# Cross-attention and FFN on one core: the second group's attention in single precision, the stacked values built later

## The reference

```
x = x + xattn(layernorm(x), ctx)        # one head of width 512, 77 keys, masked softmax
x = x + ffn(layernorm(x))

xattn: Q = q @ Wq + bq;  K = c @ Wk + bk;  V = c @ Wv + bv
       scores = Q K^T / sqrt(512), masked keys -1e9;  attn = softmax(scores)
       return (attn @ V) @ Wo + bo
ffn:   real = x @ cos(theta + theta_noise);  imag = x @ sin(phi + phi_noise)
       return sqrt(real^2 + imag^2)
```

## Time and profile before

| | us |
|---|---|
| median of 3 runs | 254.1 (252.98 to 254.43) |
| the profiled execution's own time | 254.0 |
| its span, first to last instruction | 252.2 |
| PE busy | 236.2 (94%) |
| VectorE, ScalarE, GpSimd busy | 170.4, 145.1, 55.9 |
| mean granted clock of TensorE | 0.993 of full |

### The profile page before, as it was taken

The page is one execution under the profiler, slowest core; times in us unless marked ns, Lnnn a source line. Parts: engine busy times, 40 slices in busy tenths (PEclk is TensorE's granted clock), DMA queues, the critical chain, the costliest instruction groups (busy, mean ns, idle before and its releaser), DMA issues.

```text
span 252.2 us, 3916 instructions
## 1 busy us (share of the span) xinstructions
PE 236.2 (94%) x1249; PEld 134.9 (54%) x1249; DVE 170.4 (68%) x343; ACT 145.1 (58%) x251; POOL 55.9 (22%) x152
## 2 busy tenths in 40 slices
PE   7998698868699989999999999999999999999993
PEld 2898236326244457446744674467446744444462
DVE  1774759777796686678667966796579653965452
ACT  2301863459264934893579358925892589266542
POOL 1005053340073024202320332033103310132000
PEclk9999799999999999999999999999999999999999
DMA  6999958666227772597259726872877244424522
GB/s 198 374 413 415 417 144 160 65 155 271 63 44 209 133 322 48 125 224 299 65 147 208 312 42 196 160 308 44 219 142 307 42 83 83 169 42 83 188 107 83
DMA packets 48525, 44.80 MB, mean 178 GB/s; under 512 B 42518, under 2 KB 42774, under 8 KB 45309
## 3 DMA queue, kind: packets, MB, share of 16 engines
q1 hardware_dynamic: 47557, 43.37, 57.7%
q0 software_dynamic: 288, 1.05, 2.4%
q10 hardware_dynamic: 664, 0.18, 0.3%
HBM read 25.66 MB, written 8.39 MB: 135 GB/s over the span
## 4 chain that ended last, share of the span: by engine, by line
PE 68%; DMA 12%; DVE 9%; SPq 4%; issue 3%; ACT 2%; POOL 2%; DVEq 0%; ACTq 0%; POOLq 0%
DMA wo<-in_Wo 8%; PE im L486 7%; PE re L486 7%; PE im L488 7%; PE re L488 7%; PE re L487 7%; PE im L487 7%; PE score_bank L507 6%; DMA xTb<-in_xT 4%; PE re L496 2%; PE att L461 2%; PE att L463 2%; DVE x L952 2%; PE re L520 2%; PE re L524 2%
## 5 line engine op out<-in xcount | busy, mean ns | idle before, releaser
L715 ACT ACTIVATE h<-x,shift,rstd 128x512 f32<-128x512 f32 x28 | 22.7, 810 | 36.5 <-POOL shift L371 36.5
L486 PE MATMUL im<-w_hi,hT 128*128 128x512 f16 x104 | 39.4, 379 | 2.0 <-DMA hT<-h_split 2.0
L486 PE MATMUL re<-w_hi,hT 128*128 128x512 f16 x104 | 39.4, 379 | 1.7 <-DMA hT<-h_split 1.7
L488 PE MATMUL im<-w_hi,hT 128*128 128x512 f16 x104 | 39.4, 379 | 0.0
L488 PE MATMUL re<-w_hi,hT 128*128 128x512 f16 x104 | 39.4, 379 | 0.0
L487 PE MATMUL im<-w_lo,hT 128*128 128x512 f16 x104 | 39.4, 379 | 0.0
L487 PE MATMUL re<-w_lo,hT 128*128 128x512 f16 x104 | 39.4, 379 | 0.0
L974 DVE SCALAR_TENSOR_TENSOR h_split<-h,h_split 128x512 f16<-128x512 f32 x32 | 22.1, 689 | 21.3 <-ACT h_split L719 21.2
L507 PEld LDWEIGHTS score_bank<-a_keys,xTb 128*128 128x128 f32 x160 | 29.8, 190 | 8.2 <-issue 1.4
L507 PE MATMUL score_bank<-a_keys,xTb 128*128 128x77 f32 x160 | 27.5, 254 | 0.9 <-DMA xTb<-in_xT 0.9
L952 DVE SCALAR_TENSOR_TENSOR x<-att,inv_total,xb 128x512 f32<-128x512 f32 x32 | 23.5, 735 | 3.3 <-PE att L463 2.1
(11 more groups left out here) (161 smaller groups left out, 424.0 us busy)
## 6 DMA issues: line engine op xcount, KB each, us to landing
xTb<-in_xT SPq DMA_DIRECT2D x8, 1024.0 KB, 5.0
xb<-in_x SPq DMA_DIRECT2D x8, 1024.0 KB, 5.4
out_rows<-wv SPq DMA_DIRECT2D x7, 1024.0 KB, 3.9
wk<-in_Wk SPq DMA_DIRECT2D x2, 512.0 KB, 5.4
wqT<-in_WqT SPq DMA_DIRECT2D x4, 256.0 KB, 7.4
wv<-in_Wv SPq DMA_DIRECT2D x1, 1024.0 KB, 13.5
angle_w<-in_theta SPq DMA_DIRECT2D x2, 512.0 KB, 15.2
angle_n<-in_theta_noise SPq DMA_DIRECT2D x2, 512.0 KB, 16.5
```

Of the source, the lines that this page charges most:

```text
L486: nc.tensor.matmul(bank_[:, :], hT[j][:, 0, k, :], w_hi[part][:, k, :], start=(k == 0), stop=False)
L488: last = nc.tensor.matmul(bank_[:, :], hT[j][:, 1, k, :], w_hi[part][:, k, :], start=False, stop=(k == CH - 1))
L715: nc.scalar.activation(h[j % 2][:, :], x2[b][:, j, :], ACT.Identity, bias=shift2[:, j:j + 1], scale=rstd2[:, j:j + 1]).then_inc(h_made, 1)
```

## The change

- Group 1's attention is done as group 0's: TensorE transposes `probs` (`transpose_keys`), ScalarE copies the result to `probsT`, and `attend_second` makes one single-precision matmul for each tile. `high_probs(1)`, `low_probs(1)`, the transposing DMA of `p_split` and the scaled total of group 1 are gone, and the counts in the waits of the later groups go down by one.
- ScalarE's exponentials of group 1 come before its high half of the values, which moves behind the copy and two squares.
- VectorE's low half of the values moves from before the statistics of x to behind `low_half(1, 1)`.
- On SP the transposes of h of group 1, tiles 0 and 1, come before the three copies.
- TensorE's wait for `vw_stacked` moves from before group 1's attention to before the loop.

```diff
             load_x(0, 1)
+            transpose_h(1, [0, 1])
             sp.wait_ge(vw_hi_ready, 1)
             sp.dma_start(vw_stack[1][REST - KEYS:REST, :, :],
                          vw_stack[0][0:KEYS, :, :]).then_inc(vw_stacked, 16)
             sp.wait_ge(vw_lo_ready, 1)
             sp.dma_start(vw_stack[0][KEYS:P, :, :], vw_lo[0:P - KEYS, :, :]).then_inc(vw_stacked, 16)
             sp.dma_start(vw_stack[1][0:REST - KEYS, :, :], vw_lo[P - KEYS:KEYS, :, :]).then_inc(vw_stacked, 16)
-            transpose_probs(1)
-            transpose_h(1, [0, 1])
             with sp.Fori(0, 2) as i:
...
+            def transpose_keys(m):
+
+                pe.wait_ge(probs_made, m + 1)
+                for j in range(TILES):
+                    last = nc.tensor.transpose(pT_bank[0:KEYS, P * j:P * j + P], probs[:, j, :], ident[:, :])
+                last.then_inc(pT_mm, 1)
+
+            def attend_second(j):
+
+                pe.wait_ge(pT_copied, 2)
+                pe.wait_ge(x2_made, TILES + j - 1)
+                nc.tensor.matmul(att_bank[j % 2][:, :], probsT[:, P * j:P * j + P], vw[:, 1, :],
+                                 start=True, stop=True).then_inc(att_mm, 1)
+
             def attend(m, batch, j):
 
-                pe.wait_ge(pT_ready, 16 * m)
+                pe.wait_ge(pT_ready, 16 * (m - 1))
...
             feed_first(0, 1)
-            pe.wait_ge(vw_stacked, 3 * 16)
-            attend(1, 1, 0)
-            attend(1, 1, 1)
+            pe.wait_ge(vw_norm_read, 1)
+            transpose_keys(1)
+            attend_second(0)
+            attend_second(1)
             feed_first(1, 1)
-            attend(1, 1, 2)
+            attend_second(2)
             feed_first(2, 1)
-            attend(1, 1, 3)
+            attend_second(3)
             feed_first(3, 1)
             pe.wait_ge(im_squared, 2)
+            pe.wait_ge(vw_stacked, 3 * 16)
             with pe.Fori(0, 2) as i:
...
             square_first(1, 0)
+            exps(1)
+            act.wait_ge(pT_mm, 2)
+            nc.scalar.activation(probsT[:, :], pT_bank[0:KEYS, :], ACT.Copy).then_inc(pT_copied, 1)
+            square_first(2, 0)
+            square_first(3, 0)
             act.wait_ge(vw_scale_made, 2)
             nc.scalar.activation(vw_stack[0][0:KEYS, :, :], vw[:, :, :], ACT.Copy,
                                  scale=vw_scale[0:KEYS, 0:1]).then_inc(vw_hi_ready, 1)
-            exps(1)
-            high_probs(1)
-            square_first(2, 0)
-            square_first(3, 0)
             square_first(0, 1)
...
             low_half_of_sine(1, 0)
-            dve.wait_ge(vw_hi_ready, 1)
-            nc.vector.scalar_tensor_tensor(out=vw_lo[:, :, :], in0=vw[:, :, :], scalar=vw_scale[0:KEYS, 0:1],
-                                           in1=vw_stack[0][0:KEYS, :, :], op0=ALU.mult,
-                                           op1=ALU.subtract).then_inc(vw_lo_ready, 1)
             low_half_of_sine(1, 1)
-            low_probs(1)
-            dve.wait_ge(vw_scale_made, 2)
             softmax_total(1)
...
             low_half(1, 1)
+            dve.wait_ge(vw_hi_ready, 1)
+            nc.vector.scalar_tensor_tensor(out=vw_lo[:, :, :], in0=vw[:, :, :], scalar=vw_scale[0:KEYS, 0:1],
+                                           in1=vw_stack[0][0:KEYS, :, :], op0=ALU.mult,
+                                           op1=ALU.subtract).then_inc(vw_lo_ready, 1)
             residual(1, 1, 3)
```

More of the change, by code:

```diff
@@ L267, in transpose_probs @@
             def transpose_probs(m):
-                sp.wait_ge(p_lo_made, m)
+                sp.wait_ge(p_lo_made, m - 1)
                 sp.sem_inc(transposes_sent, 1)
@@ L699, in high_probs @@
                 act.wait_ge(probs_made, m + 1)
-                if not isinstance(m, int) or m > 1:
-                    act.wait_ge(pT_ready, 16 * (m - 1))
+                if not isinstance(m, int) or m > 2:
+                    act.wait_ge(pT_ready, 16 * (m - 2))
                 nc.scalar.activation(p_split[:, :, 0:2 * KEYS].rearrange("p t (s k) -> p t s k", s=2),
@@ L929, in softmax_total @@
                 dve.wait_ge(probs_made, m + 1)
-                if not isinstance(m, int) or m > 0:
+                if not isinstance(m, int) or m > 1:
                     nc.vector.tensor_scalar(scaled_total[:, :], total[:, :], total_scale[:, 0:1], None,
                                             ALU.mult).then_inc(total_scaled, 1)
-                    dve.wait_ge(total_scaled, m)
+                    dve.wait_ge(total_scaled, m - 1)
                     dve.wait_ge(x2_made, TILES * m)
@@ L936, in softmax_total @@
                 else:
+                    if m > 0:
+                        dve.wait_ge(x2_made, TILES * m)
                     nc.vector.reciprocal(inv_total[:, :], total[:, :]).then_inc(inv_total_made, 1)
             def low_probs(m):
-                dve.wait_ge(p_hi_made, m)
+                dve.wait_ge(p_hi_made, m - 1)
                 nc.vector.scalar_tensor_tensor(out=p_split[:, :, 2 * KEYS:STACK], in0=probs[:, :, :], scalar=P_SCALE,
```

## The result

| | before | after |
|---|---|---|
| median, us | 254.26 (252.98 to 256.11, 4 runs) | 260.33 (259.44 to 261.99, 4 runs) |
| ratio, 95% interval | | 1.024 (1.016 to 1.032) |
| profiled execution, us | 254.0 | 262.0 |
| its span, us | 252.2 | 260.2 |
| PE busy, us | 236.2 | 241.7 |

The kernel is 2.4% slower, 6.1 us by the medians; 5.9 were forecast, 259.9 us. All medians here are of all runs of a kernel, while the ratios leave out the few runs in a slower state, over 1.5% above the fastest of the same kernel. The profiled execution of after is the longest of its four, so its 262.0 stands above the median by 1.7 us; what the trace says is compared from stage to stage, not from start to end.

The account below looks back on a forecast made before the run. From the loop's start on, only PE's own work was taken to set the time. Added to 254.0 us: later loop start +5.4, closed xTb gap -0.9, clock +1.4, giving 259.9 us, range 257.0 to 261.8.

Parts of the forecast that it names:

- Attention ahead of the loop: Group 1's attention on PE: transposes at 65.08, then ScalarE's copy, attention at 66.36 us against 67.18 before.
- PE at the loop: PE, with 2.5 us more work, reaches the loop at 77.8 us, 1.1 later than before.
- SP's order: On the SP queue, the three value copies go out behind the transposes of h, at 77.2, 78.2 and 79.0 us.
- Landing: The second value copy, 51 partitions, lands last, 3.7 us after its issue, at 81.9; bounds put the loop at 81.1 to 84.3.
- The loop's start: PE waits for the stack and starts its loop at 82.1 instead of 76.69 us, +5.4, idling 4.3.
- Where the shift is not given back: Loads and tiles behind the copies, about 1 to 2.6 us later, stay covered by PE's later loop start.
- the wait for xTb: PE's 0.88 us wait in the loop closes, since xTb is there at 92.7 and wanted at 96.3: -0.9 us.
- The clock: TensorE's clock falls to 0.50 behind the new idle time near 82 us, costing +1.4 us; bounds 0 and about 3.
- The sum: Whole kernel: +5.4 - 0.9 + 1.4 = +5.9 us on 254.0, so 259.9 us.
- The clock stays up: Rival at the loop's entry: the same stall without the clock's fall, 258.5 us; chance 0.17.
- The clock stays low for longer: Rival behind the stall: clock cost of 3 us, 261.5 us; chance 0.12, shared with a late stack, 262.1.
- The cover holds: Rival: the copies land before PE reaches the loop, which starts at 77.8; 254.2 us, not slower; chance 0.08.

Follow-up runs that it names:

- e7: e1 with the transposes of h put in front of the three value copies on SP again; 262.1 us, one run.
- e8: The changed kernel with only SP's order undone, copies before the transposes of h, halves still made late; 258.6 us, one run.
- e1: The changed kernel with the value halves made early and their copies first on SP again; 254.4 us, ratio 1.0002 to the kernel before.
- e4: The changed kernel with the copy of 51 partitions split into 48 and 3; 258.2 us, one run.
- e2: The changed kernel with PE's wait for the stack moved from before the loop to the loop's attention; 257.02 us, ratio 1.0105 to before.
- e3: The changed kernel with 22 unused matmuls ahead of PE's wait for the stack; 258.5 us, ratio 1.0157 to before.
- e9: e5 with 12 unused matmuls ahead of the wait for wo; 252.04 us, ratio 0.9912 to the kernel before.
- e10: The kernel before with 12 unused matmuls ahead of PE's wait for wo; 253.34 us, ratio 0.9969 to before.
- e11: e9 with 8 more unused matmuls ahead of feed_first(0, 0); 252.69 us, ratio 0.9953 to the kernel before.
- e6: e2 with the copy of 51 partitions also split into 48 and 3; 256.13 us, ratio 1.0107 to the kernel before.
- e5: e1 with group 1's transposes of the probabilities moved ahead of feed_first(0, 1); 253.64 us, ratio 1.0006 to the kernel before.

## Why the prediction was right, step by step

**Attention ahead of the loop.** Forecast in two steps: transposes one slot behind the last matmul, attention 1.28 us behind them, at 66.36. In the trace the transposes start 0.22 us after that matmul, the copy 0.64 later (66.34, 0.59 long), and the attention 1.28 after the transposes, at 66.98; the 0.61 us of difference were there before. VectorE's first residual came 1.17 us behind the attention's start (68.15), as group 0 had shown. Group 0's own rows were enough to size this part.

**PE at the loop.** Forecast 77.8. The last matmul ahead of the loop starts at 78.08, so PE is through at 78.3; less the 0.61 us by which this execution was late above, it is 77.7.

**SP's order.** Forecast 77.2, 78.2 and 79.0 for the copies, measured 77.55, 78.60 and 79.35: 0.35 to 0.4 later as the trace stands, 0.2 to 0.3 earlier when the 0.61 are taken off. e7 shows that this order alone makes the whole stall. That VectorE's halves were made in time held: `vw_lo` was done at 77.37, before the second copy's turn at 78.60. e8 shows what the prediction had only in half a sentence: VectorE's low half of the values, which it called not last, would be last as soon as the queue isn't.

**Landing.** This was the least certain term: 3.7 us after the issue of the 51-partition copy, from a DMA share of 0.20. By the chain the stack was there at 82.64, 4.0 us after 78.60. Where nothing else moves bytes the reading comes out as forecast: in e1 the copy is issued at 65.66, and the DMA share is 0.06 up to 69.20 and 0.00 behind it, 3.5 us later. The Trainium skill (DMA: Bandwidth & Descriptors, "Anatomy of one DMA") would have put it 0.8 us before my figure; the chain puts it 0.3 behind it. The Trainium skill gives that fit for DMAs that GpSimd issues, and these are issued by SP, so this case isn't a test of it. The Trainium skill's rule for the number of engines (same page, "Why a DMA increments its semaphore by 16 and not by 1") fits e4: with 48 partitions in place of 51 the last copy is followed by the loop after 2.67 us and not 3.74. Going into the loop took 0.45 us from the landing, where 0.1 to 0.3 had been set.

**The loop's start.** Forecast 82.1, +5.4. It was 83.09, +6.4, of which 0.6 came from above: +5.8. The missing 0.4 are the landing (0.3) and the entry (0.25), less 0.2 by which the second copy was earlier than forecast.

**Where the shift is not given back.** Rightly, the wait for xTb (0.9) closed. The claim that all else behind the copies is covered held, though not by the figures given for it: xTb, "1 us later now at the worst", was issued at 89.88, 3.1 us later (2.5 without the 0.6 from above). It was there 4.9 us later at 94.8, and PE took it at 100.0 because the stall was longer and the clock low. In e2, where PE doesn't stall, the same queue makes PE wait 1.18 us for pT and 0.96 for xTb: a queue 2.6 us later was counted, but not that the load behind the 3-engine copy also gets slower (7.8 us in place of 5.65, e4) and that the transposes stay on the queue until that load is over (3.03 us in place of 1.44).

**The clock.** The direction was right, and in the traced execution it is the term that was mis-sized: 1.4 us forecast, with the 3.4 us of the earlier trace rows as a model. The clock was low for 6.8 us (about 82.2 to 89.0). From the loop's start to the end of the span after has 177.1 us (260.2 - 83.09), e3 174.3 (257.3 - 82.97): 2.8 us, near the upper bound of 3. But the size isn't fixed by the idle time. In e7 (4.70 us idle) it is 6.8 us and 177.1 again; in e8 (4.64) and e4 (4.18) the clock was low for 3.4 us, as in the model, and 175.8 and 175.5 us follow the loop's start, 1.5 and 1.2 over e3. So two traces have the forecast's size and two have twice that. By the medians (e3) it is 1.8.

**The sum.** In the traced execution: 0.6 from above, 5.8 for the loop's start, -0.9 for xTb, 2.5 to 2.8 for the clock, 8.0 to 8.3 where the spans differ by 8.0. The median of after, 260.33, is 0.4 above the forecast. Since the traced execution is 1.7 us above that median, the near miss is partly luck: the terms of this one trace would give 261.7 without the time from above (254.0 + 5.8 - 0.9 + 2.8). With 1.4 for the clock they give 260.3, the median. The likely reason for the lower median is therefore the clock, besides the spread of the first 60 us. Where the clock fell in the other three runs isn't recorded, but their mean granted clock is 0.983 to 0.984, against 0.979, and e8, whose trace has one low stretch of 3.4 us behind the stall and one at 43 us, has 0.983 too. That is argued, not shown.

**The rivals.** "The clock stays up" (258.5) fell by the trace, and e3 gave what it would be, 258.5. "The clock stays low for longer" (261.5) is what the traced execution shows: its terms give 261.7. The median doesn't show it. "The cover holds" (254.2) is what e1 measures once the copies are early, 254.4: its mechanism was right and its condition not met.

## What to carry to other kernels

A wait belongs where the data is used: put ahead of a loop, it sits on the loop's branch and holds work that doesn't need the data (3.3 us here by the medians, e2, part of it the clock's). When a transfer is moved on a queue, ask both what it now waits behind and what waits behind it, and undo making and sending together, since either alone keeps the other's delay (e7, e8). Where an idle time of some microseconds on TensorE can't be removed, cheap matmuls in it can keep the clock up and the loss to the idle time itself (e3). Look for where the clock falls next (e9, e10), and expect nothing where another engine or queue is the bound (e11). And compare the clock's cost over several traces: behind the same idle time it differed by a factor of two here.

## What the runs showed of the hardware

- PE idle for 4.63 us (after) and 4.70 us (e7) came with 6.8 us at the lower clock, for 4.64 us (e8) and 4.18 us (e4) with 3.4 us; filled with matmuls, with none (e3).
- The clock behind PE's idle time at 24 to 27 us isn't the same from execution to execution. It fell after 2.72 (before), 2.98 (after), 2.79 (e1), 2.88 (e3), 2.98 (e6) and 3.04 (e7) us, and stayed at 1.00 after 2.23 (e2), 2.45 (e5) and 2.51 (e8), but also after 2.96 (e4). In e5, e8, e9 and e10, where it stayed up or the idle time was filled, it fell instead at 43 to 45 us, around a wait of 1.28, 1.44, 2.23 and 2.12 us, while e2 and e4 kept it through 1.46 and 1.57 us there. The rows don't say what decides. Filling it narrowed the runs from 253.1 to 255.7 (before) to 252.8 to 254.2 (e10).
- A copy of 51 partitions, 102 KB, ran on few engines (DMA share 0.20) and landed 3.5 us (e1, last bytes) to at most 4.0 us (after) after its issue. A load of x of 1 MB issued 2 us behind it was in after 7.3 (e2) to 8.5 us (e3), where 5.5 are seen 4.7 us behind it (e8) and 5.6 and 5.5 behind the split copy (e4, e6).
- The transposing DMA of the probabilities, issued while the load of 1 MB ahead of it was still under way, stayed on the queue until 0.1 to 0.2 us before that load was in: 1.30 us (e6), 1.44 (e4), 2.36 (e8), 2.57 (e2), 3.03 (after), 3.72 (e3), 4.61 (e7). Where the load was in before, it took 1.23 us (before, e1, e5).
- From the landing of the last awaited DMA to the first matmul behind a loop's branch it took 0.45 us.
